# Scanning a recurrence over pairs of time steps, with the decay and the sums on two other engines

## What is computed

```
attn      = softmax(q k^T / 4 + causal mask);  y_softmax = attn v
retention = 1 - sigmoid(Lambda_raw)                       # one number for each (head, i, j)
step:  state = retention * state + Gamma * (v_t outer k_t/4);   y_t = (W_static + state) q_t
y = alpha * y_softmax + (1 - alpha) * y_stp;   x = x + y @ out_w + out_b
x = x + ffn_fp8(layernorm(x))
```

## Time and profile before

| | us |
|---|---|
| median of 3 runs | 2258.62 (2258.2 to 2261.62) |
| span of the profiled execution | 2262.8 |
| attention, group by group | 465.5, 464.1, 461.3, 426.2 |
| busy in the span: PE, DVE, ACT, POOL | 2012.1, 1911.7, 1258.6, 838.2 |

### The profile page before, as it was taken

The page is one execution under the profiler, slowest core; times in us unless marked ns, Lnnn a source line. Parts: engine busy times, 40 slices in busy tenths (PEclk is TensorE's granted clock), DMA queues, the critical chain, the costliest instruction groups (busy, mean ns, idle before and its releaser), DMA issues. The chain is left out here.

```text
span 2262.8 us, 42161 instructions
## 1 busy us (share of the span) xinstructions
PE 2012.1 (89%) x11840; PEld 696.9 (31%) x11840; DVE 1911.7 (84%) x3051; ACT 1258.6 (56%) x2518; POOL 838.2 (37%) x843
## 2 busy tenths in 40 slices
PE   6876999999989999999898999989999999998543
PEld 3441233323323332333223333232332322222432
DVE  5656999998997999989987999898979898863677
ACT  3532166665655666666556666665656666766221
POOL 1320042433443433425342424253514242754435
PEclk9985599999999999999999999999999999999775
DMA  5987152251132622512235314221452111211702
GB/s 142 266 188 168 23 95 49 66 88 57 44 82 56 103 64 57 90 49 62 59 71 101 73 50 67 68 62 53 88 79 75 47 45 38 68 44 35 198 28 74
DMA packets 153963, 179.50 MB, mean 79 GB/s; under 512 B 62352, under 2 KB 100240, under 8 KB 153744
## 3 DMA queue, kind: packets, MB, share of 16 engines
q1 hardware_dynamic: 151360, 175.06, 33.2%
q10 hardware_dynamic: 2384, 1.77, 0.3%
HBM read 134.32 MB, written 42.21 MB: 78 GB/s over the span
## 5 line engine op out<-in xcount | busy, mean ns | idle before, releaser
L1004 DVE TENSOR_REDUCE pmax<-PS 128x1 f32<-128x512 f32 (+3 forms) x2304 | 1335.1, 635 | 181.9 <-PE PS L860 123.2
L971 ACT ACTIVATE probs<-PS 128x512 f32<-128x512 f32 (+3 forms) x2304 | 1118.0, 567 | 615.3 <-PE PS L878 481.6
L860 PE MATMUL PS<-K_st,Q_st 96*128 96x512 bf16 (+3 forms) x1408 | 502.3, 362 | 32.9 <-DVE pmax L1004 28.9
L878 PE MATMUL PS<-Q_st,K_st 98*128 98x512 bf16 (+3 forms) x1408 | 443.2, 361 | 16.5 <-ACT probs L971 11.3
L824 POOL COPY carry<-state 128x1 f32<-128x1 f32 x256 | 47.1, 184 | 1061.9 <-DVE state L1040 1061.9
L860 PE MATMUL PS<-K_first,Q_st 96*128 96x512 bf16 (+3 forms) x896 | 354.2, 411 | 64.9 <-DVE pmax L1004 34.0
L835 POOL TENSOR_TENSOR v_exp<-v_exp,k_rows 128x512 f32<-128x512 f32 x256 | 348.2, 1361 | 108.4 <-DMA v_exp<-qkv_t 108.2
L1040 DVE TENSOR_TENSOR_SCAN state<-retention,carry,v_exp 128x512 f32<-128x512 f32 x256 | 357.1, 1395 | 1.8 <-POOL v_exp L835 1.6
L899 PE MATMUL PS<-probs,V_g 128*17 128x512 f32 (+3 forms) x2816 | 343.5, 561 | 0.0
L826 POOL TENSOR_TENSOR state<-state,q_rows 128x512 f32<-128x512 f32 x256 | 330.5, 1291 | 20.6 <-POOL carry L824 0.2
L878 PE MATMUL PS<-Q_st,K_first 98*128 98x512 bf16 (+3 forms) x896 | 298.7, 373 | 7.2 <-issue 6.2
(11 more groups left out here) (124 smaller groups left out, 999.0 us busy)
## 6 DMA issues: line engine op xcount, KB each, us to landing
v_exp<-qkv_t SPq DMA_DIRECT2D x256, 256.0 KB
qkv_t<-proj SPq DMA_DIRECT2D x24, 512.0 KB, 3.5
qk_parts<-parts SPq DMA_DIRECT2D x24, 512.0 KB, 4.7
Q_st<-qk_parts SPq DMA_DIRECT2D x192, 64.0 KB, 3.9
K_first<-qk_parts SPq DMA_DIRECT2D x24, 320.0 KB, 12.6
K_st<-qk_parts SPq DMA_DIRECT2D x24, 320.0 KB, 13.6
K_st<-qk_parts SPq DMA_DIRECT2D x24, 192.0 KB, 6.8
v_rows<-vaug SPq DMA_DIRECT2D x32, 136.0 KB, 5.9
```

Of the source, the lines that this page charges most:

```text
L860: mm = pe.matmul(PS[:, bank, 0:width], Q_st[0:KS, c, h, j * P:(j + 1) * P], keys[0:KS, h, blk * CH:blk * CH + width], start=True, stop=(bl ...
L878: mm = pe.matmul(PS[:, bank, 0:CH - r * P], keys[:, h, kt * P:(kt + 1) * P], Q_st[:, c, h, r * P:CH], start=True, stop=(kt < TPC * c))
L971: act.activation(probs[:, tile % P_SLOTS, h, 0:CH - r * P], PS[:, item % S_BANKS, 0:CH - r * P], ACT.Exp, scale=SCALE).then_inc(exp_done, 1)
L1004: dve.tensor_reduce(pmax[:, s % 2, hj, blk:blk + 1], PS[:, S_BANKS + item % M_BANKS, 0:width], AX.X, ALU.max).then_inc(max_done, 1)
```

## The change

The recurrence is rewritten for pairs of steps. With decay r, s_(2m) = r*r * s_(2m-2) + (r * u_(2m-1) + u_(2m)), and the skipped states are filled in as s_(2m+1) = r * s_(2m) + u_(2m+1). For each unit:

- ScalarE (`scale`) writes r * u of the even columns to a new buffer `pairs`; GpSimd (`add_pairs`) adds u of the odd ones and copies the carry ahead of them;
- VectorE scans the 257 columns of `pairs` with `retention_sq` into every second column of `state`, which has one column more;
- ScalarE (`decay`) writes r * state into the columns between; GpSimd (in `weigh`) adds u to them, saves the carry and multiplies by q as before.

In the list, unit n is preceded by `decay` of unit n - 1 and followed by `scale` of unit n + 1; of the three empty slots behind 16 units the first holds the last `decay`, and one slot is put ahead of unit 0, so that units stand one or two tiles later than before and the dense part has 28 units still (36 to 63). GpSimd takes product of n + 1, `add_pairs` of n, `weigh` of n - 1. The ring of `v_exp` is 8 deep, and SP waits for `weighted` where it waited for `scanned`. The last four tiles stay free.

```diff
-RING = 4
+RING = 8
+PAIR = CH // 2
...
-        slots += [("unit", b * BURST + i) for i in range(BURST)] + [None] * 3 + [("burst", b)]
+        slots += [("unit", b * BURST + i) for i in range(BURST)] + [("decay", (b + 1) * BURST - 1), None, None, ("burst", b)]
+    slots.insert(0, ("scale", 0))
...
-                    emit(("unit", 0, item[1]), event=False)
+                    n = item[1]
+                    if n % BURST:
+                        emit(("decay", 0, n - 1), event=False)
+                    emit(("unit", 0, n), event=False)
+                    if n + 1 < UNITS:
+                        emit(("scale", 0, n + 1), event=False)
...
-                                    sp.wait_ge(scanned, g * UNITS + s + 1)
+                                    sp.wait_ge(weighted, g * UNITS + s + HALF * HD)
...
+                    def add_pairs(g, n):
...
+                        pool.wait_ge(u_scaled, g * UNITS + n + 1)
+                        pool.tensor_tensor(pairs[:, n % 2, 1:], pairs[:, n % 2, 1:], v_exp[:, n % RING, 1:CH:2], ALU.add)\
+                            .then_inc(pair_made, 1)
+                        pool.wait_ge(carried, g * UNITS + n + 1)
...
+                        pool.tensor_copy(pairs[:, n % 2, 0:1], carry[:, col:col + 1]).then_inc(pair_made, 1)
...
+                        pool.wait_ge(decayed, g * UNITS + n + 1)
+                        pool.tensor_tensor(state[:, i, 1:CH + 1:2], state[:, i, 1:CH + 1:2], v_exp[:, n % RING, 0:CH:2],
+                                           ALU.add).then_inc(evened, 1)
+                        pool.tensor_copy(carry[:, col:col + 1], state[:, i, CH:CH + 1]).then_inc(carried, 1)
...
+                            if n + 1 < UNITS:
+                                product(g, n + 1)
+                            add_pairs(g, n)
                             if n >= 1:
                                 weigh(g, n - 1)
...
+                            elif kind == "scale":
...
+                                act.wait_ge(u_made, g * UNITS + s + 1)
+                                act.wait_ge(scanned, g * UNITS + s + 1)
+                                act.activation(pairs[:, s % 2, 1:], v_exp[:, s % RING, 0:CH:2], ACT.Identity,
+                                               scale=retention[:, col:col + 1]).then_inc(u_scaled, 1)
+                            elif kind == "decay":
...
+                                act.wait_ge(scanned, g * UNITS + s + 3)
+                                act.activation(state[:, i, 1:CH + 1:2], state[:, i, 0:CH:2], ACT.Identity,
+                                               scale=retention[:, col:col + 1]).then_inc(decayed, 1)
...
-                                dve.wait_ge(u_made, g * UNITS + s + 1)
+                                dve.wait_ge(pair_made, g * (2 * UNITS) + 2 * s + 2)
...
-                                dve.tensor_tensor_scan(state[:, i], retention[:, col:col + 1].broadcast_to([P, CH]),
-                                                       v_exp[:, s % RING], carry[:, col:col + 1], ALU.mult, ALU.add)\
+                                dve.tensor_tensor_scan(state[:, i, 0:CH + 1:2],
+                                                       retention_sq[:, col:col + 1].broadcast_to([P, PAIR + 1]),
+                                                       pairs[:, s % 2], 0.0, ALU.mult, ALU.add)\
```

More of the change, by code:

```diff
@@ L179, in group_steps @@
                 if item and item[0] == "unit":
-                    emit(("unit", 0, item[1]), event=False)
+                    n = item[1]
[4 more added lines that the diff above has]
+                        emit(("scale", 0, n + 1), event=False)
+                elif item and item[0] in ("scale", "decay"):
+                    emit((item[0], 0, item[1]), event=False)
                 elif item:
@@ L190, in group_steps @@
             done = total - len(todo) - done
-            n = max(n - done, 0)
-            share = [n * (i + 1) // 5 - n * i // 5 for i in range(5)]
+            due = max(due - done, 0)
+            share = [due * (i + 1) // 5 - due * i // 5 for i in range(5)]
             for h in range(GH):
@@ L252, in preln_attention_ffn_kernel @@
         retention = sb("retention", [P, HALF * HD])
+        retention_sq = sb("retention_sq", [P, HALF * HD])
         sum_j = sb("sum_j", [P, HALF, HD, VW])
@@ L655, in _ @@
                     link(dve.tensor_scalar(retention[:, :], lam_sb[:, :], -1.0, 1.0, ALU.mult, ALU.add))
+                    link(dve.tensor_tensor(retention_sq[:, :], retention[:, :], retention[:, :], ALU.mult))
                     link(dve.memset(carry[:, :], 0.0))
@@ L714, in preln_attention_ffn_kernel @@
             v_exp = sb("v_exp", [P, RING, CH], where=att)
-            state = sb("state", [P, BURST, CH], where=att)
+            pairs = sb("pairs", [P, 2, 1 + PAIR], where=att)
+            state = sb("state", [P, BURST, 1 + CH], where=att)
             stp_sb = sb("stp_sb", [P, 2, CH], where=att)
@@ L817, in _, with product @@
                 def _(pool):
-                    def weigh(g, n):
-                        pool.wait_ge(scanned, g * UNITS + n + 2)
+                    def product(g, n):
+                        b = n // BURST
+                        if n % BURST == 0:
+                            pool.wait_ge(kq_loaded[b % 2], g * 64 + 32 * (b // 2) + 32)
+                        pool.wait_ge(vexp_loaded[n % RING], g * (16 * UNITS // RING) + 16 * (n // RING) + 16)
+                        pool.tensor_tensor(v_exp[:, n % RING], v_exp[:, n % RING], k_rows[:, b % 2], ALU.mult)\
+                            .then_inc(u_made, 1)
@@ L919, in burst @@
                                 mm = pe.matmul(PS[q * VW:(q + 1) * VW, 7, :], sum_j[:, half, i, :],
-                                               state[:, i], start=False, stop=(k == TPC - 1))
+                                               state[:, i, 1:], start=False, stop=(k == TPC - 1))
                             if k == TPC - 1:
@@ L1057, in preln_attention_ffn_kernel @@
             xn2 = sb("xn2", [P, NT, D], where=fin)
+            alpha = sb("alpha", [P, NT, H], where=fin)
             soft = sb("soft", [P, 2, TPC, D], where=fin)
```

28 lines of the change are left out of this document (15 added, 13 removed).

## The result

The changed kernel takes 2298.94 us (median of 4, 2293.62 to 2301.66), the kernel before 2260.12 beside it (4 runs, 2258.2 to 2264.89): a ratio of 1.0158, with a 95% interval of 1.0135 to 1.0181. It is 1.6% slower; 2284 was forecast, 1.1%. The profiled execution spans 2299.9 us where it spanned 2262.8, so 37.1 us are to be found.

The account below looks back on a forecast made before the run. TensorE and VectorE were held near full in groups 0 to 2, VectorE slack in group 3. Terms 6 - 22 + 22 - 5 + 24 = +25 us on 2262.8 gave 2288, median 4 lower: 2284 us, range 2255 to 2320.

Parts of the forecast that it names:

- Scan: VectorE's scan of 257 columns: 0.71 us forecast, between 0.64 and 0.84, saving some 0.5 us a unit where nothing blocks it.
- First 88 tiles: Tiles 0 to 87 of each group: shorter scans return half of 11 us, 4 x -5.5 = -22 us.
- GpSimd's additions: GpSimd's two additions of 256 columns a unit: 0.73 us each, 0.70 back to back.
- dear-additions rival: Slower rival: strided GpSimd additions cost 1.27 us each, 5.9 us a unit; dense parts pay +115, total 2399; chance 0.09.
- Collisions: Scans inside GpSimd's chain shut GpSimd out: 0.45 us a unit, raising 4.35 to 4.8 us.
- ScalarE: `scale` and `decay` at 0.50 us each just fit ScalarE's pause ahead of a tile; 0.025 us a unit, +6 us.
- rival (2330): Slower rival: ScalarE becomes the bound, exponentials start 0.2 us late for 256 units, 51 in place of 6; chance 0.11.
- Dense part, groups 0 to 2: Tiles 88 to 139: VectorE waits for late pairs, 5.0 us a unit; 7.5 us more a group, +22 us.
- fewer collisions: Tiles around the priced runs of the dense parts gain 5 us over all groups.
- Dense part, group 3: Tiles 88 to 139, where VectorE has slack: GpSimd at 4.8 us a unit without a pause is the bound, +24 us.
- GpSimd over 90% busy: Sign that the forecast is right: GpSimd's busy share in group 3's dense part, with that part near 170 us.
- GpSimd keeps pace: Faster rival: at 4.2 us a unit GpSimd isn't late in groups 0 to 2; sum -52, 2207; chance 0.22.

## Why the prediction was right, and where it was not

The direction and the size held: 2298.9 against 2284, in the forecast's own range of 2255 to 2320. The size held in part by luck: the gain was put at 22 us and is 39, the losses at 47 (ScalarE's 6 among them) and are 73.5 in the dense parts and the last four tiles, and the two errors go against each other. By its steps:

- **Scan.** 0.71 us was worked out for 257 columns; the changed kernel's scans have 671 ns at least and 726 by the median:

```profile
L1087 DVE TENSOR_TENSOR_SCAN state<-retention_sq,pairs x256: 671/726/1600, 285.9 to 2101.4; 128x257 f32<-128x257 f32 x128
```

  Writing every second column was put at nothing, and that held: the half scan, 256 adjacent columns, has a median of 742.

- **First 88 tiles: right in kind, half in size.** I had worked out a floor of 263 us from TensorE's pace and then took half of the 11 us above it, -22 in all. The four groups came to 264.2, 263.5, 263.7 and 262.5: all of it, -39.4. The half had no row behind it. The run with the half scan alone gave 263.9 in group 1, as good as the same.
- **GpSimd's additions.** 0.73 forecast, 739 and 855 ns measured by the mean. The dear-additions rival (1.27 each) fell. The second addition has its destination and both inputs at every second column; it costs 0.84 unblocked, 0.1 more than the other. A chain without collision was put at 4.35 us and measured 4.32. The prediction weighed what the Trainium skill, "GPSIMD Engine Reference", section "Performance pitfalls for Q7 kernels", says of steps of more than 8 bytes; the trace agrees so far that no half again appears at exactly 8.
- **Collisions.** 0.45 us a unit was taken; the saturated cycle above has 4.71 - 4.32 = 0.39, all of it in the one-column copy (0.58 instead of 0.18). On average over the dense stretches it is less, 4.6 - 4.32, some 0.3. Collisions could not be taken away by themselves, so what they cost in the whole is not separated. The two runs that moved them (without the additions, and GpSimd's work with the long scan) show that each engine pays for the length of the other's instruction, as the Trainium skill says under "SBUF — State Buffer", section "SBUF: two separate sides"; the trace agrees down to a copy of one column (0.58 and 1.11 us in place of 0.18).
- **ScalarE.** +6 us forecast, some +4 measured with the two instructions alone; 536 and 544 ns each in the changed kernel where I had 0.50. As a rival (2330) it fell. But the step named only VectorE's wait for the pairs as the route of the loss. `scale` stands ahead of four exponentials and waits for GpSimd's product of the next unit, and this cost ScalarE 77.6 us of waiting. I had written "If they cost 0.59, or wait, ScalarE's tile is late", and then charged nothing for the waiting. Taking that one wait away returned 17 us, net of the wait for the scan that came instead.
- **Dense part, groups 0 to 2.** 5.0 us a unit forecast, 5.12 and 4.93 measured in group 1. The two stretches that were priced came out as priced: 5.4 us more from unit 36 to 47, and 74.0 - 15 x 4.77 = 2.4 from 48 to 63 over the same tiles, 7.8 together against 7.5. Yet the dense part pays 10.8. The other 3 us a group lie around the two stretches, before unit 36, where unit 35 now stands too, and between 47 and 48, where I had forecast a gain of 5 in all ("fewer collisions") without a row that shows one. So +22 - 5 was +33.9.
- **Dense part, group 3.** The failed step is "GpSimd at 4.8 without a pause is the bound", +24; measured were +33.9, at 5.0 us a unit. The words that fail are "without a pause". GpSimd works 4.6 us a unit there and waits 0.2 to 0.5 for `decay`. That the work binds was half right: with two slots ahead the pauses are gone, GpSimd still takes 4.6, and the part still costs 19.4 (167.2 against 147.8). The other 14.5 us came back with the lead alone, on the same instructions. I had the lead in the text, used it in groups 0 to 2, and dropped it in group 3 for a simpler bound. That 4.8 came near 5.0 is luck: the collisions were put too high by some 0.15 and the pauses at nothing. The sign I gave, GpSimd over 90% busy, did not suit my own sum, as 28 units at 4.8 are 134 us, 79% of 170. Over the whole part it was 133.5 of 181.7, 73%; in the stretches between scans above it was 51.3 of 54.5 and 65.4 of 75.4, 94% and 87%.
- **The last four tiles.** +5.7 us in all, not priced. The prediction looked at loads and SP's wait and left the tiles behind the last unit alone. In group 1 the four tiles take 13.9 us before and 16.0 after; with two slots ahead 14.1, with that and a spread of 0.54 14.4, and of 0.585 15.6. The trace shows the next chunk's shift issued later (L803, L790 before): 10.9 us behind the start of tile 140 in place of 9.7. It moves with the list, but by what rule stays open.
- **GpSimd keeps pace** (the faster rival, 2207, decided below some 4.4 us a unit). Its number came true in the run with two slots ahead and an even spread, 2214, but not its condition: GpSimd's work is 4.6 us a unit in that run too, and it keeps pace because the units stand 4.7 to 5.2 us apart. Where they stood closer, with the old spread, it did not keep pace even with the lead.

## What to carry to other kernels

When work moves to an engine with room, work out when each of its results is wanted and when its input exists, and not only whether it fits: here the same instructions cost +1.6% with a lead of one slot and brought -0.9% with two. Then compare its work for a unit with the distance of the units in the densest stretch, and not over the whole: spread to suit, the same instructions brought -2.1%. A small instruction that waits at the head of an in-order queue costs everyone behind it, so its wait is charged to the large work that follows, not to the small one. And try a change of schedule on the kernel before as well, as it has a price of its own: the even spread cost the kernel before 29 us and the changed one 3, and brought 30 once the lead was there.

## What was not expected of the hardware

- A GpSimd copy of one column, 128x1, takes 0.18 us unblocked, 0.58 beside a scan of 0.7, and 1.11 beside a scan of 1.28. The exclusion goes by the other's length, not by one's own size, so splitting work into small pieces does not avoid it.
- On GpSimd, 256 columns with every operand at a distance of 8 bytes take 0.84 us instead of 0.73.
- Taking work off an engine can lengthen what is left: without the two additions the product rose from 1.28 us to 1.56 by its mean and the scan from 0.89 to 1.13, as most scans now began under a multiplication of 512 columns and held up the product behind it.
- The granted clock in group 3's dense part fell to 0.91 of 2.4 GHz (0.99 before), and to 0.82 between units 48 and 63, so for a good third of that time to 1.2 GHz, after a stretch in which TensorE stood idle at the slots, up to 2.5 us at once. With two slots ahead and the even spread it was 0.98. The pace of the units was 4.96 us at 0.94 and 5.03 at 0.82, and with the product two units ahead 4.65 at 1.00 and 4.68 at 0.85, so the clock did not set it; whether it cost something between the runs, no run tells.
